# Attention with mixture-of-experts on one core: where a two-way branch is taken, and which row groups are loaded before a block ends

## The reference

```
x = x + cross_attention(context, layernorm(x), mask)     # 16 heads of 64, q and k RMS-normalised with gains qn_g, kn_g
    ln = layernorm(layernorm(x)), xn = layernorm(context)
    q = ln @ Wq ; k, v = [xn ; ln] @ Wkv ; softmax(q k^T / 8) v ; @ Wout + bout
h = layernorm(x)
x = x + shared_ffn(h) + sum over the 2 best of 8 experts of gate * ffn_e(h)   # hidden size 1024, gelu
```

## Time and profile before

| | us |
|---|---|
| median of 3 runs | 2508.64 (2507.91 to 2509.59) |
| the profiled execution's own time | 2505.31 |
| its span | 2503.8 |
| PE busy | 2408.4 (96%) |
| DVE busy | 1749.3 (70%) |
| ACT busy | 1689.1 (67%) |
| POOL busy | 1212.2 (48%) |

### The profile page before, as it was taken

The page is one execution under the profiler, slowest core; times in us unless marked ns, Lnnn a source line. Parts: engine busy times, 40 slices in busy tenths (PEclk is TensorE's granted clock), DMA queues, the critical chain, the costliest instruction groups (busy, mean ns, idle before and its releaser), DMA issues. The chain is left out here.

```text
span 2503.8 us, 53762 instructions
## 1 busy us (share of the span) xinstructions
PE 2408.4 (96%) x19926; PEld 1997.1 (80%) x19926; DVE 1749.3 (70%) x2452; ACT 1689.1 (67%) x2286; POOL 1212.2 (48%) x783
## 2 busy tenths in 40 slices
PE   4899999999999999999999999988989999999997
PEld 3677777777777777777777777658989999999997
DVE  7666766676667666766676667777875567777775
ACT  2688888888888888888888888872333345444443
POOL 5444434443445344534453445425515537677766
PEclk9899999999999999999999999998999999999999
DMA  6423332323333323233333232247804279999996
GB/s 199 148 84 115 100 98 86 124 92 100 94 115 100 101 85 123 91 100 94 115 99 101 86 123 90 68 125 167 200 10 144 92 243 320 317 327 317 319 326 166
DMA packets 231532, 363.25 MB, mean 145 GB/s; under 512 B 59559, under 2 KB 139739, under 8 KB 227400
## 3 DMA queue, kind: packets, MB, share of 16 engines
q1 hardware_dynamic: 204694, 301.66, 39.2%
q0 software_dynamic: 25696, 58.82, 8.1%
q10 hardware_dynamic: 978, 0.34, 0.1%
HBM read 280.90 MB, written 79.85 MB: 144 GB/s over the span
## 5 line engine op out<-in xcount | busy, mean ns | idle before, releaser
L734 DVE TENSOR_TENSOR pr_lo<-ps_s,pr_hi 128x1024 fp32r<-128x1024 f32 x420 | 513.0, 1221 | 297.2 <-ACT ps_s L844 297.2
L843 ACT ACTIVATE pr_hi<-ps_s 128x1024 fp32r<-128x1024 f32 x512 | 527.4, 1030 | 133.5 <-PE ps_s L991 110.1
L476 POOL TENSOR_TENSOR rs<-ss,minus_half 128x16 f32<-128x16 f32 (+1 forms) x96 | 226.8, 2362 | 555.4 <-DVE ss L709 555.4
L1700 ACT ACTIVATE ht<-f_ps_h,b 128x256 f32<-128x256 f32 x440 | 184.6, 471 | 338.8 <-PE f_ps_h L1632 338.8
L1027 PE MATMUL ps_o<-pr_hi,vA 64*65 64x512 f32 x1780 | 378.2, 391 | 2.5 <-DVE pr_lo L734 2.5
L1027 PE MATMUL ps_o<-pr_lo,vA 64*65 64x512 f32 x1780 | 377.2, 390 | 0.0
L1027 PE MATMUL ps_o<-pr_hi,vC 64*65 64x512 f32 x1780 | 376.5, 390 | 0.0
L844 ACT ACTIVATE ps_s<-ps_s 128x1024 f32<-128x1024 f32 x360 | 370.9, 1030 | 0.0
L1632 PE MATMUL f_ps_h<-xT_hi,w 128*128 128x256 f32 x1760 | 353.5, 284 | 3.3 <-DVE xT_lo L1734 2.3
L957 PE MATMUL ps_m<-w_sb,lnT_sb 64*128 64x384 f32 (+1 forms) x3072 | 326.0, 335 | 11.7 <-POOL w_sb L532 4.8
L1645 PE MATMUL f_ps_y<-w,h_hi 128*128 128x256 f32 x1760 | 325.6, 283 | 0.0
(11 more groups left out here) (220 smaller groups left out, 4698.3 us busy)
## 6 DMA issues: line engine op xcount, KB each, us to landing
w<-w1S_dram SPq DMA_DIRECT2D x160, 512.0 KB, 6.2
lnT_sb<-lnT_dram SPq DMA_DIRECT2D x31, 2304.0 KB, 8.9
w2raw<-in_L_ffn_Wproj SPq DMA_DIRECT2D x78, 512.0 KB, 7.0
w1S_dram<-cut POOLq DMA_DIRECT2D x36, 512.0 KB, 3.0
rec<-rden_dram SPq DMA_DIRECT2D x63, 256.0 KB, 3.7
routed_dram<-empty POOLq DMA_DIRECT2D x28, 387.0 KB, 3.5
xt<-routed_dram SPq DMA_DIRECT2D x39, 258.0 KB, 6.7
w_raw<-in_L_xattn_Wkv SPq DMA_DIRECT2D x66, 128.0 KB, 2.9
```

The source lines that it names most:

```text
L476: g.tensor_tensor(rs[:, 0:sums], ss[:, 0:sums], minus_half[:, 0:sums], ALU.pow).then_inc(s_pool, 1)
L734: v.tensor_tensor(pr_lo[:, ring(w, d), :], full_of(w, d), pr_hi[:, ring(w, d), :].bitcast(F32), ALU.subtract).then_inc(s_lo, 1)
L843: act.activation(pr_hi[:, ring(w, d), :], ps_s[:, d % 2, :], ACT.Exp, bias=bias)
L1700: ins = act.activation(ht[:, p, i, :], ps_h[:, p % 2, i, :], ACT.Gelu_apprx_tanh, bias=b1[:, slot, p, i:i + 1])
```

## The change

Three edits are made together. The two bodies of the branch swap places: the general one now follows the branch, and the bounded one is reached by a jump and ends the block's code. VectorE's choice moves to the front: it waits for the two gains (a semaphore of their own, `s_gain`) right after its four first memsets, and its whole opening (`start`), PE's first transposes and ACT's first scalings move into the bodies, behind the branch. In the last window SP also loads row group 2, each of the loads has a semaphore of its own that `project_out` waits for, and the wait at the end of attention goes. In `project_out` the hand-made `s_lop` increment becomes POOL's first instruction, groups 0 to 2 of batch 0 are not loaded, and the steps of the small sums move: ACT's fetch of "den" behind the high parts of group 1, its second detour and DVE's multiplication from q = 1 to q = 2.

```diff
-            with eng.If(eng.value_load(bounded[0:1, 0:1], min_val=0, max_val=1) > 0):
+            with eng.If(eng.value_load(bounded[0:1, 0:1], min_val=0, max_val=1) < 1):
+                body(True)
+            with eng.Else():
                 body(False)
-            with eng.Else():
-                body(True)
...
                 if closing(w) and w.s == 1:
                     sp.wait_ge(c_lo, 2)
-                    carry.load_a(sp, attT, 0, 1, c_a1)
+                    carry.load_a(sp, attT, 0, 1, carry.s_rows[0])
+                    sp.wait_ge(c_lo, 4)
+                    carry.load_a(sp, attT, 0, 2, carry.s_rows[1])
...
-            sp.wait_ge(c_a1, 32)
...
             v.memset(mrow[:, :, :].bitcast(F32), 0.0).then_inc(s_const, 1)
+            dve.wait_ge(s_gain, 32)
+            v.scalar_tensor_tensor(gqk[:, :], gq[:, :], DH ** 0.5, gk[:, :], ALU.mult, ALU.mult).then_inc(s_const, 1)
+            dve.wait_ge(s_const, 5)
+            compared = [0]
+            step(dve, s_bound, compared, v.tensor_tensor(gain2[:, :], gqk[:, :], gqk[:, :], ALU.mult))
+            step(dve, s_bound, compared, v.tensor_reduce(most2[:, :], gain2[:, :], AX.X, ALU.max))
+            step(dve, s_bound, compared, v.tensor_scalar(bounded_f[:, :], most2[:, :], MOST ** 2, None, ALU.is_le))
+            step(dve, s_bound, compared, v.tensor_copy(bounded[:, :], bounded_f[:, :]))
...
+            def start():        # pads, statistics(0), centre(0), gain_col, masks, split(0, j), statistics(1)
...
+                start()
                 windows(dve, window)
...
-            upper_w(0, 1)
-            act.wait_ge(p_g, 64)
-            for j in range(PREPS):
-                scaled(0, j)
-            act.wait_ge(s_const, 6)
-            either(act, lambda general: windows(act, window))
+            def act_windows(general):
+                upper_w(0, 1)
+                act.wait_ge(p_g, 64)
+                for j in range(PREPS):
+                    scaled(0, j)
+                act.wait_ge(s_const, 6)
+                windows(act, window)
+
+            either(act, act_windows)
...
             def pe_windows(general):
+                pe.wait_ge(s_id, 2)
+                for j in range(PREPS):
+                    prep(0, j)
+                pe.wait_ge(s_const, 6)
...
-                    if b == 0 and q < 2:
-                        sp.sem_inc(s_a[q], 32)
-                    else:
+                    if b > 0 or q > 2:
                         carry.load_a(sp, attT, b, q, s_a[q])
...
         def _(pool):
+            pool.sem_inc(s_lop, 1)
...
-            act.wait_ge(s_put, 16)
-            act.dma_start(den[:, :], last.rearrange("h (p k) -> p (h k)", p=P)).then_inc(s_den, 16)
...
                     if b == 0 and q == 1:
+                        act.wait_ge(s_put, 16)
+                        act.dma_start(den[:, :], last.rearrange("h (p k) -> p (h k)", p=P)).then_inc(s_den, 16)
+                    if b == 0 and q == 2:
                         act.wait_ge(s_inv, 1)
...
-                    if b == 0 and q == 1:
+                    if b == 0 and q == 2:
                         dve.wait_ge(s_rec, 16)
```

More of the change, by code:

```diff
@@ L133, in __init__ @@
     def __init__(self, t):
+        self.s_rows = [t.sem("c_rows1"), t.sem("c_rows2")]
         self.lnT_sb = t.sb("lnT_sb", [P, 2, C, KEYS], F32R)
@@ L220, in attention @@
         p_st, p_first, p_lnT, p_pad, p_wipe = (t.sem("p_" + n) for n in ("st", "first", "lnT", "pad", "wipe"))
+        s_gain = t.sem("a_gain")
         s_id, s_g, s_const = t.sem("a_id"), t.sem("a_g"), t.sem("a_const")
@@ L231, in attention @@
         s_den, s_inv, s_put, s_rec, s_norm = (t.sem("a_" + n) for n in ("den", "inv", "put", "rec", "norm"))
-        c_wo, c_a0, c_a1, c_hi, c_lo = (t.sem("c_" + n) for n in ("wo", "a0", "a1", "hi", "lo"))
+        c_wo, c_a0, c_hi, c_lo = (t.sem("c_" + n) for n in ("wo", "a0", "hi", "lo"))
         s_zero, s_clear = t.sem("a_zero"), t.sem("a_clear")
@@ L589, in split @@
                 v.tensor_tensor(lower, f, upper.bitcast(F32), ALU.subtract).then_inc(p_split, 1)
[L591 to L622, removed]
-            for j in range(PREPS):
-                split(0, j)
-            statistics(1)
+            def start():
+                for b in (0, 1, B - 1):
+                    for part in range(2):
+                        for c in range(C):
+                            v.memset(prepared(b, part, c)[:, N + CTX:KEYS].bitcast(F32), 0.0).then_inc(p_wipe, 1)
+                statistics(0)
+                dve.wait_ge(p_c, 16)
+                for b in range(B):
+                    v.bn_stats(cstats[0:CTX, b, :], cz[:, b, :]).then_inc(p_st, 1)
+                dve.wait_ge(p_st, 2 * NT + B)
+                for b in range(B):
+                    v.bn_aggr(cmv[0:CTX, b, :], cstats[0:CTX, b, :]).then_inc(p_st, 1)
+                dve.wait_ge(p_st, 2 * NT + 2 * B)
+                v.tensor_scalar(cvar_eps[0:CTX, :], cmv[0:CTX, :, 1], 1.0, LN_EPS, ALU.mult, ALU.add).then_inc(p_ve, 1)
+                centre(0)
+                dve.wait_ge(p_rs, 2)
+                for b in range(B):
+                    v.tensor_scalar(cz[:, b, :], cz[:, b, :], cmv[0:CTX, b, 0:1], crstd[0:CTX, b:b + 1],
+                                    ALU.subtract, ALU.mult).then_inc(p_z, 1)
+                dve.wait_ge(s_g, 64)
+                v.scalar_tensor_tensor(gain_col[:, :], gq_col[:, :], DH ** 0.5, gk_col[:, :], ALU.mult, ALU.mult).then_inc(s_const, 1)
+                dve.wait_ge(p_m, 32)
+                v.tensor_scalar(mkf[:, :], mk8[:, :], -NEG, NEG, ALU.mult, ALU.add).then_inc(p_mk, 1)
+                v.tensor_scalar(mrf, mr8[:, :], -NEG, NEG, ALU.mult, ALU.add).then_inc(p_mk, 1)
+                for j in range(PREPS):
+                    split(0, j)
+                statistics(1)
@@ L854, in window @@
                         opening(w, d)
-            act.dma_start(gq[:, :], qn_g.rearrange("(a d) -> a d", a=1).broadcast_to([P, DH])).then_inc(s_g, 16)
-            act.dma_start(gk[:, :], kn_g.rearrange("(a d) -> a d", a=1).broadcast_to([P, DH])).then_inc(s_g, 16)
+            act.dma_start(gq[:, :], qn_g.rearrange("(a d) -> a d", a=1).broadcast_to([P, DH])).then_inc(s_gain, 16)
+            act.dma_start(gk[:, :], kn_g.rearrange("(a d) -> a d", a=1).broadcast_to([P, DH])).then_inc(s_gain, 16)
             for half in range(2):
@@ L871, in _ @@
             mm = nc.tensor.matmul
-            pe.wait_ge(s_id, 2)
             def prep(b, j):
@@ L901, in opening @@
                         prep(3, d - 8)
-            for j in range(PREPS):
-                prep(0, j)
-            pe.wait_ge(s_const, 6)
             def turn(w, i):
@@ L1244, in batch @@
                     free(act, s_y, b * G + q - 1)
-                    act.wait_ge(s_a[q], b * 32 + 32)
+                    if b > 0 or q > 2:
+                        act.wait_ge(s_a[q], (b + (q > 2)) * 32)
+                    elif q > 0:
+                        act.wait_ge(carry.s_rows[q - 1], 32)
                     if b == 0 and q == 0:
```

1 line of the change is left out of this document (removed).

## The result

The changed kernel takes 2518.29 us in the median of 9 runs (2512.38 to 2522.43) against 2508.64 (2506.53 to 2509.59): a ratio of 1.0037, interval 1.0028 to 1.0046, some 9.7 us slower. Beside the last two experiments it took 2520.46 against 2509.24, ratio 1.0048 (1.0034 to 1.0061). The direction was the forecast one; the size was more than double.

The account below looks back on a forecast made before the run. DVE's chain was taken to bound the opening, and DVE's and POOL's pace project_out, with PE working 96% of the span. Start +6.0 and seam −1.8 gave +4.2 us: median 2508.64 becomes 2512.8, range 2505.5 to 2517.0.

Parts of the forecast that it names:

- the start: Opening, where all hangs on DVE's statistics: choice and jump now come first; net +6.0 us (+3.7 to +8.1), carried on whole.
- the jump's size: DVE's jump to the general body at the start: 5.0 us, near PE's branch, bounds 2.7 and 6.7.
- the price of "a group later": project_out: SP stores o_second before loading batch 1, so that load comes late; of 5.9 us lead about 1.8 are left.
- the seam: Between attention and project_out: last group's shift −1.8 us, bounds 0 (late load eats all) and −5.9 (lands in time).
- What is saved between centring and split: Opening, between the centring's end and DVE's first split: of 1.73 us, 0.5 stays; 1.2 us saved.
- The seam's start: Start of project_out: block begins 5.4 us earlier, x rows land behind group 2, DVE's first addition 5.9 us earlier.
- The fetch of "den": project_out, after ACT's work on group 1: back at 1697 when DVE needs it; nothing, up to 1 us if late.
- The third row group: Loaded early in attention, it saves its own load in project_out, but ACT waited there for PE; worth nothing.
- Both at the dear end: Rival: jump 6.7 us, register loads 1.6, late load eats the lead; +8.1, 2516.7 us; chance 0.16.
- The seam keeps its gain: Rival: batch 1's load lands within the slack, −5.9 instead of −1.8; +0.1 in all, 2508.7 us; chance 0.12.
- The cheap jump: Rival: the jump at the start costs nearly nothing (0.1 us), start +1.1; −0.7 in all, 2507.9 us; chance 0.10.
- the fast small loads: Rival: group 0's x rows overtake the group load at project_out's start, lead up to 9.8 us; −6.1, 2502.5; chance 0.12.

Follow-up runs that it names:

- the last two experiments: Changed kernel with DVE's jump late on empty queues, sums at old groups, o_second stored in batch 1: 2505.09 us; the same without the third row group's early load: 2506.05.
- Experiment 7: Changed kernel, but VectorE alone keeps the bounded body first, the other four engines jumping early: 2510.68 us, ratio 1.0011 to the kernel before.
- experiment 2: Changed kernel, but SP stores o_second in batch 1 behind group 1's loads instead of ahead of them: 2511.95 us, ratio 1.0014 to the kernel before.
- experiments 1 and 7: The first of the pair: changed kernel with the two bodies back in their old order, bounded first: 2513.97 us, ratio 1.0018 to the kernel before.
- Experiment 3: Changed kernel, but SP issues the 1 MB of x's second batch only after DVE's jump: 2515.95 us, ratio 1.0028 to the kernel before.
- experiment 9: Changed kernel, but SP, POOL, ACT unbranched, DVE's jump inside the second attention-free window, small sums at old groups, o_second stored in batch 1: 2505.09 us, ratio 0.9982.
- experiment 6: Changed kernel without the third row group's load in attention; group 2 is loaded in project_out as before: 2515.02 us, ratio 1.0023 to the kernel before.
- experiments 2 and 5: The second of the pair: changed kernel with the small sums back at their old groups: 2509.92 us, ratio 1.0007 to the kernel before.

## Why the prediction was right in kind and wrong in size

**The bound, and the start as the place of the loss: right.** DVE's jump was named as the term, with statistics 7.2 us late; they were 9.96 late. Experiment 7 shows that DVE's jump alone did it, and that PE's and ACT's are hidden, which I had costed at nothing.

**Two terms of the sum failed, the jump's size and the price of "a group later".** The start was put at +6.0 and measured +8.4 at the first split, the seam at −1.8 and measured +1.9 at the last addition; another +1.5 inside attention and −1.7 in the experts were not in the sum.

**The jump.** I took 5.0 us, "near PE's, since the first transfers are nearly done by then", and gave 6.7 as the upper bound. It was 8.9. The choice was ready 0.9 us earlier than I had it, and the jump fell deeper into the loads; in experiment 2, where it began 1.5 us later, it took 6.1. The upper bound was wrong in kind: 6.7 us was no limit of a jump but what one row group in the queues had made of it, and experiments 1 and 7 show 7.8 and 8.1 behind two. The trace of before had the full share at 10 to 13 us in front of me. Experiment 3 (1 MB taken out of the queue, 3.1 us gained) and experiment 9 (empty queues, 2.8 us) show the cost following the queue. The Trainium skill's sentence ("Runtime: NRT & Kernel Launch", Instruction fetch mechanics) on a stall for a target outside the window fits all nine rows and the `instruction` packets; none of the rows fits the Trainium skill's 0.1 us ("Advanced Engine Details and Errata", Control Flow Timing). One reading was wrong there: of ACT's two records, 56 ns is the branch that falls through at 27.7 and 38 ns is the far jump at 1679.5, behind which ACT drains 2.7 us later. So a short record does not show a near branch.

**What is saved between centring and split: nearly right,** 1.5 us instead of 1.2 (+9.96 at the statistics, +8.44 at the split). Another 1.5 us arose between the split and attention's last copy (+9.98), and not steadily: the changed kernel's shift is 7.9 us at 75 us, 5.9 at 83 and 9.3 at 95 (times of the kernel before). Other kernels differ there by −1.3 (experiment 7) to +2.9 us (experiment 6), so I leave that open.

**The seam's start: right within 0.2 us.** Predicted: the first addition 5.9 us earlier, behind group 2 in SP's queue. It came 5.8 us earlier, POOL waiting 7.83 us for the rows of x. The fetch of "den" was costed at "nothing, up to 1 us"; it landed at 1707.9, just about with the rows of x, and experiment 6 shows it as the next wait, so it was no more covered than by chance.

**The price of "a group later": right in mechanism, half its size.** I had ACT waiting "2 to 4 us" for batch 1's first load and the lead shrinking from 5.9 to 1.8. ACT waited 9.82 us, and the lead of 5.8 became a loss of 1.9. Three things were off. From group 1 on the additions had 0.8 to 0.9 us less lead than I gave them (3.9 instead of 4.8 at group 2), so group 3 kept 0.6 and not 1.8. For group 4 my own figures, POOL's low parts at 1728.5 and 6 us of product, give 1734.5 against 1735.77 before: a lead of 1.3, where I wrote 1.8. And that product took longer than 6 us. It began at 1739.90 after 7.20 us of idleness and the addition came 7.8 us later, at 1747.70; PE's next step came 7.5 us after it began, where the product before had taken 5.8 (1725.48 to 1731.32). The granted clock was 1.00 of full from 1727 to 1732, the level of 2.4 GHz, and 0.53 from 1740 to 1744, nearly all at 1.2 GHz, and DVE stood 4.23 us before the addition. The window:

```profile
1740.00:1744.00 4.00, 4.00 (x20) 4.00 (x21) 2.83 (x3) 2.00 (x2) 2.71 (x3) 0.53 0.82 170
```

Experiments 2 and 5 take SP's wait away in two ways and return 5.1 and 6.8 us. The third row group was priced at nothing; with the late sums it costs some 2 us (experiment 6).

**The rivals.** "Both at the dear end" (2516.7, chance 0.16) was the nearest and still 1.6 us short. "The seam keeps its gain" is the direction in which experiments 2 and 5 go, with leads of 3.2 and 4.8 us at the last addition, not 5.9. The cheap jump and the fast small loads did not occur. The range ended at 2517.0 because its upper end was built from a cost seen once and taken for a maximum.

## What to carry to other kernels

A branch to a body that does not follow it is a transfer, as the `instruction` packets here show: before placing it, look at what stands in the transfer queues at that moment and not only at whether the engine idles. Here the same jump cost 2.8 us on empty queues and 8.9 among the first loads. When small steps are moved a group later, ask which in-order queue waits for their last one and what it issues next. And a duration seen once under load bounds nothing from above until one knows what it waited for.

## What the runs showed of the hardware that was not expected

A branch's own record does not tell its cost on every engine: DVE's says 67 ns with 8.9 us of nothing behind it, PE's says 6984 ns. The three engines that jumped at the start in the changed kernel came through at 17.7 (ACT), 19.0 (DVE) and, by its record, 16.8 (PE), although their branches lay within 0.3 us. The changed kernel's nine runs spread over 10.0 us (2512.4 to 2522.4), those of the kernel before beside them over 3.1; but the kernel before spread over 4.6 to 8.6 us in its longer series, so the spread is not shown to be the jump's.
